# A redrawn opening: weights between the pieces of x on one load queue, and half of the token work moved into the loop

## The chip, the core and the metric

The kernel runs on one core of a Trainium2 chip. The metric is the device time of one execution in microseconds. The core has a matrix engine (PE, with its weight loads shown as PEld), a vector engine (DVE), a scalar engine (ACT), a general engine (POOL) and a queue engine (SP) that here issues all DMA transfers. Each engine runs its own instruction list in order, and waits on semaphores for the others.

## What is computed

One block of a Perceiver-like network on x (32 batches, 32 tokens, 256 features) with a context of 257 rows per batch. In float32:

```python
y  = layernorm(x)
Q  = y @ Wq.T + bq;  K = ctx @ Wk.T + bk;  V = ctx @ Wv.T + bv     # 16 heads of 16
x1 = x + (softmax(mask(Q K^T / 4)) V) @ Wo.T + bo
x2 = x1 + causal self attention with rotary positions (W_Q, W_K, W_V, W_O) of layernorm(x1)
out = x2 + top-2 mixture of 8 experts (gated, hidden 1368) of layernorm(x2)
```

The shapes and the use of x, of the context and of the eight square weights are what matters here. The expert part is not touched by the change.

## The kernel before, in words

The 1024 tokens are 8 tiles (TT) of 128 rows, 4 batches to a tile. Each float32 matrix product is made as three products (product3, lines 215 to 217) of a high and a low part: a transposed operand lands in a bank of PSUM, ACT rounds it into the high part, and DVE subtracts to get the low part.

The program has an opening, a loop of 8 steps (j) with 4 units (u) each, one unit for each batch b = 4j + u, a stage that routes tokens, and a stage for the experts. The change touches the opening and the first two steps of the loop.

**The opening before.** SP issues, in this order: the constant table, the four pieces of x (x_sb, 256 KB each), the first three weights (w_raw: Wq and Wk in two pieces of 128 KB each, because their rows are regrouped by head, lines 336 and 337; Wv in one), the last context rows, the three biases, the context of batches 0 to 3, bo, the mask, the other five weights, the router. PE takes a list of slots, each in one of 8 banks: the bias (line 435), the weights 0 to 2 (line 440), the last context rows (line 459), their keys and values (kl, vl), the four pieces of normed tokens (xT, line 446), and four query products (q) of 512 columns. ACT copies every slot (lines 935 to 949), and DVE makes the low parts of weights, last rows and tokens (line 1245). DVE clears three buffers first, then makes the statistics of all 8 tiles (lines 1250 to 1255), and POOL takes the power -0.5 (line 1756). DVE norms all tiles (line 1261). POOL adds bo to x (line 1761). Only after all slots are done does the context of batch 0 go through PE: turn_ctx (line 491), keys, values, then turn_ctx for batch 1.

**The loop before.** Unit b starts with energies(b) (line 534), then turns the context of b + 2, makes the keys of b + 1, turns probabilities of b - 1 (line 556), makes the values of b + 1, and in units 0 to 2 of step 0 turns two late weights (line 592), which ACT and DVE split (lines 954 and 1272). values(b + 1) waits until ACT has kept the keys (line 971), since both use bank 5. The scores of a unit are shifted by DVE (line 1296), exponentiated by ACT (line 994), and scaled by POOL (line 1799).

**vl.** The values of the last context row are stored to memory and read back eight times with a broadcast (VL_all, line 387, 1 MB written in all). SP issues the context of batch 4 only behind that.

## Time and profile before

| | |
|---|---|
| median of 3 runs | 563.48 us (556.87 to 567.03) |
| the profiled execution | 566.69 us, of which the trace spans 564.8 us |
| busy share of the span | PE 89%, DVE 72%, ACT 58%, POOL 44% |
| first energies (start of the loop) | 45.05 us after the span's start |
| PE busy in 0 to 45.05 us | 23.57 us |
| PE busy in 45.05 to 297 us | 237.20 of 251.95 us |

An execution's time is the span and some 2 us around it. PE is busy nearly all the time from the loop on, but only about half of the opening. A row of the timeline gives start, duration, engine, line, operation, output and inputs, shape and count, and in brackets how long the engine had been idle before it and what ended that. A row of the windows gives the stretch, its length, the busy time of each engine with the number of instructions, the granted PE clock (PEclk), the mean busy share of the 16 DMA engines and the GB/s moved.

### The profile page before, as it was taken

Reading aid. Unit: us, or ns where it says so; the run is one execution under the profiler, and the core shown is the slowest. Engines: PE = TensorE matmul, PEld = TensorE weight load, DVE = VectorE, ACT = ScalarE, POOL = GpSimd, SP = SyncE. Lnnn points to the kernel's source line nnn. Section 1 sums busy time; section 2 is a strip of 40 time slices with the busy share of each in tenths; the row PEclk is TensorE's granted clock in tenths of the full one; section 3 lists DMA queues with packets and bytes.
Section 4 is the critical chain, followed back from the end, with each engine's and each line's share of the span. In section 5 each row is a group of like instructions: output and inputs, shape, how many; then the busy total and the mean of one; then the engine's idle time right before and its main releaser. Section 6 shows DMA issues by size and latency. Waiting matters only on the chain.

```text
span 564.8 us, 18262 instructions
## 1 busy us (share of the span) xinstructions
PE 501.6 (89%) x6637; PEld 460.1 (81%) x6637; DVE 406.2 (72%) x1005; ACT 325.1 (58%) x839; POOL 247.3 (44%) x337
## 2 busy tenths in 40 slices
PE   0777999989999999999976657899999999999996
PEld 0656778878889898888865546799999999999995
DVE  6414346477666767676676788599999999999973
ACT  0325667577667757676752215666665766657650
POOL 1301153344445364444430120366667667676650
PEclk9989899999999999999996765599999999999998
DMA  7420111121111111120006200055655656465302
GB/s 217 129 94 19 38 43 40 27 55 22 42 39 35 26 33 38 21 54 2 4 2 200 102 0 1 5 196 167 188 158 189 198 174 195 146 187 188 113 1 74
DMA packets 57981, 48.91 MB, mean 87 GB/s; under 512 B 20926, under 2 KB 49600, under 8 KB 57920
## 3 DMA queue, kind: packets, MB, share of 16 engines
q1 hardware_dynamic: 57920, 48.09, 28.9%
q8 instruction: 39, 0.64, 0.5%
q14 instruction: 22, 0.18, 0.1%
HBM read 46.86 MB, written 1.08 MB: 85 GB/s over the span
## 4 chain that ended last, share of the span: by engine, by line
PE 77%; ACT 7%; DVE 5%; issue 5%; DMA 2%; SPq 2%; POOL 0%; DVEq 0%; ACTq 0%; POOLq 0%
PE bank L215 20%; PE bank L217 18%; PE bank L216 18%; PE bank L556 5%; PE bank L534 3%; PE bank L580 3%; ACT Pr L994 2%; PE bank L491 2%; PE bank L925 2%; PE bank L711 1%; ACT PTd L1087 1%; DMA bias_raw<-in_L_xattn_bv 1%; PE bank L673 1%; DMA last_prob<-Pr 1%; PE bank L684 1%
## 5 line engine op out<-in xcount | busy, mean ns | idle before, releaser
L215 PE MATMUL bank<-XT_lo,W_hi 128*128 128x256 f32 (+1 forms) x352 | 100.5, 286 | 1.3 <-ACT CT L1166 1.3
L216 PE MATMUL bank<-XT_hi,W_lo 128*128 128x256 f32 (+1 forms) x352 | 100.1, 284 | 0.0
L217 PE MATMUL bank<-XT_hi,W_hi 128*128 128x256 f32 (+1 forms) x352 | 99.8, 284 | 0.0
L1876 POOL TENSOR_TENSOR W_lo<-raw,W_hi 128x256 fp32r<-128x256 f32 (+1 forms) x88 | 88.4, 1005 | 7.0
L1799 POOL TENSOR_TENSOR Pr<-Pr,rinv 128x1028 f32<-128x1028 f32 x31 | 58.9, 1901 | 51.1 <-DVE rinv L1307 50.4
L994 ACT ACTIVATE Pr<-Sc,nmax 128x257 f32<-128x257 f32 x128 | 63.8, 502 | 23.1 <-DVE nmax L1296 21.6
L1296 DVE CUSTOM_DVE_ANT_0 Sc<-bank,mask_add 128x257 f32<-128x257 f32 x128 | 46.9, 422 | 38.8 <-PE bank L534 16.8
L1738 DVE TENSOR_TENSOR hid_lo<-hid,hid_hi 128x256 fp32r<-128x256 f32 (+1 forms) x88 | 73.1, 831 | 1.5 <-ACT hid_hi L1215 1.5
L1708 DVE TENSOR_TENSOR W_lo<-raw,W_hi 128x512 fp32r<-128x512 f32 (+1 forms) x88 | 68.8, 784 | 5.2 <-ACT W_hi L1139 1.4
L1874 POOL CAST W_hi<-raw 128x256 fp32r<-128x256 f32 (+1 forms) x88 | 39.1, 444 | 74.3 <-PE bank L217 36.9
L215 PEld LDWEIGHTS bank<-XT_lo,W_hi 128*128 128x128 f32 (+1 forms) x352 | 66.6, 189 | 1.6 <-issue 1.6
L216 PEld LDWEIGHTS bank<-XT_hi,W_lo 128*128 128x128 f32 (+1 forms) x352 | 66.4, 189 | 0.0
L217 PEld LDWEIGHTS bank<-XT_hi,W_hi 128*128 128x128 f32 (+1 forms) x352 | 66.3, 188 | 0.0
L1211 ACT ACTIVATE act<-bank 128x256 f32<-128x256 f32 (+1 forms) x88 | 33.7, 383 | 53.9 <-PE bank L217 53.3
L1139 ACT ACTIVATE W_hi<-raw 128x512 fp32r<-128x512 f32 (+1 forms) x88 | 53.6, 612 | 0.0
L215 PE MATMUL bank<-W_lo,hid_hi 128*128 128x256 f32 (+1 forms) x176 | 49.7, 282 | 0.5 <-issue 0.5
L216 PE MATMUL bank<-W_hi,hid_lo 128*128 128x256 f32 (+1 forms) x176 | 49.5, 281 | 0.0
L217 PE MATMUL bank<-W_hi,hid_hi 128*128 128x256 f32 (+1 forms) x176 | 49.5, 281 | 0.0
L1215 ACT ACTIVATE hid_hi<-hid 128x256 fp32r<-128x256 f32 (+1 forms) x88 | 36.9, 419 | 14.2 <-DVE hid L1733 12.3
L1733 DVE TENSOR_TENSOR hid<-bank,act 128x256 f32<-128x256 f32 (+1 forms) x88 | 36.4, 414 | 11.8 <-ACT act L1211 11.5
L215 PE MATMUL bank<-WT_lo,ctxT_hi 128*128 128x256 f32 x128 | 40.1, 314 | 4.7 <-ACT KT L971 4.5
L215 PE MATMUL bank<-ctxT_lo,WT_hi 128*128 128x256 f32 x128 | 39.4, 308 | 1.5 <-DVE ctxT_lo L1281 1.5
(234 smaller groups left out, 1333.4 us busy)
## 6 DMA issues: line engine op xcount, KB each, us to landing
raw<-in_L_ffn_w_kernel SPq DMA_DIRECT2D x32, 512.0 KB, 4.6
ctx_raw<-in_ctx SPq DMA_DIRECT2D x32, 256.0 KB, 2.8
raw<-in_L_ffn_wo_kernel SPq DMA_DIRECT2D x16, 512.0 KB, 5.8
raw<-in_L_ffn_w_kernel SPq DMA_DIRECT2D x16, 344.0 KB
last_prob<-Pr SPq DMA_DIRECT2D x128, 1.0 KB, 1.8
raw<-in_L_ffn_wo_kernel SPq DMA_DIRECT2D x8, 256.0 KB
x_sb<-in_x SPq DMA_DIRECT2D x4, 256.0 KB, 3.9
VL_all<-vl_rows SPq DMA_DIRECT2D x8, 128.0 KB
```

The lines of the kernel that those rows point to most:

```text
L215: pe.matmul(dst, a_hi, b_lo, start=first, stop=False)
L216: pe.matmul(dst, a_lo, b_hi, start=False, stop=False)
L217: return pe.matmul(dst, a_hi, b_hi, start=False, stop=last)
L994: ac.activation(Pr[:, r % 2, g, 0:SC], Sc[:, r % 2, g, 0:SC], ACT.Exp, bias=nmax[:, r % 2, g:g + 1], scale=-1.0, accum_out=Pr[:, r % 2, g, ...
L1139: ac.activation(W01_hi[:, (NT * half_ + n) % RW, :, :, 0:w].rearrange("p i k n -> p (i k) n"), raw01[:, :, :, t * P:t * P + w].rearrange(" ...
L1215: ac.activation(hid_hi[0:w, m % RW, :], hid[0:w, m % RH, :], ACT.Copy).then_inc(sm["hhi_done"], 1)
L1296: ve.tensor_tensor_reduce(Sc[:, r % 2, g, 0:SC], bk[g][:, 0:SC], mask_add[:, :], -0.25, 3e38, ALU.add, ALU.min, nmax[:, r % 2, g:g + 1]).t ...
L1708: ve.tensor_tensor(W01_lo[:, (NT * half_ + n) % RW, :, :, 0:w].rearrange("p i k n -> p (i k) n"), raw01[:, :, :, t * P:t * P + w].rearrang ...
L1738: ve.tensor_tensor(hid_lo[0:w, m % RW, :], hid[0:w, m % RH, :], f(hid_hi[0:w, m % RW, :]), ALU.subtract)\
L1799: po.tensor_tensor(Pr[:, r % 2, :, 0:SC], Pr[:, r % 2, :, 0:SC], rinv[:, r % 2, :].unsqueeze(2).broadcast_to([P, G, SC]), ALU.mult).then_i ...
L1874: po.tensor_copy(W2_hi[0:w, m % RW, :], raw2[0:w, t, :]).then_inc(sm["hi2"], 1)
L1876: po.tensor_tensor(W2_lo[0:w, m % RW, :], raw2[0:w, t, :], f(W2_hi[0:w, m % RW, :]), ALU.subtract)\
```

## The change

All loads stay on SP, but in another order: the identity part of the table alone, Wq, x pieces 0 and 1, Wk, the biases, the context of batch 0, Wv, the last rows, the rest of the table, the context of batch 1, the mask, x pieces 2 and 3, and so on.

The list of slots is shorter and in another order. Only tokens 0 to 511 (x pieces 0 and 1) are normed, turned and projected in the opening. The context of batch 0 is turned behind the first two weights, and its keys are made behind the third. The slots use six banks. The other half of the tokens is done by functions called late (PE, ACT, DVE) in unit 3 of step 0 and unit 0 of step 1. values(0) is made inside unit 0, behind energies(0). DVE no longer clears V, PTd and Vm: POOL does. POOL adds bo to x two tiles per unit of step 0. The late weights are turned ahead of values(b + 1) and no longer behind, and ACT splits them ahead of keep_values.

```diff
-    slots = [("bias", 0)] + [("w", i) for i in range(WF)] + [("lastT", 0), ("kl", 0), ("vl", 0)]
-    slots += [("xT", c) for c in range(4)] + [("q", c) for c in range(4)]
+    slots = [("w", 0), ("w", 1), ("bias", 0), ("lastT", 0), ("xT", 0), ("xT", 1), ("w", 2), ("q", 0), ("q", 1), ("kl", 0), ("vl", 0)]
+    ROOM = (0, 1, 2, 3, 6, 7)
...
+    def late_tokens(j, u, part):
+        return {(0, 3, 0): (0,), (0, 3, 1): (1,), (1, 0, 0): (2,), (1, 0, 1): (3,)}.get((j, u, part), ()) if isinstance(j, int) else ()
...
             elif kind == "vl":
+                pe.wait_ge(sm["first_act"], n)
+                pe.wait_ge(sm["first_dve"], sum(by_dve[:n]))
...
+        def late(n):
+            pe.wait_ge(sm["w_lo"], 8 - WF)
+            if n < 2:
+                pe.wait_ge(sm["lx_lo"], n)
+                turn_tokens(2 + n, bk[6]).then_inc(sm["lx_made"], 1)
+            else:
+                pe.wait_ge(sm["lx_hi"], 2)
+                pe.wait_ge(sm["lx_lo"], 2)
+                pe.wait_ge(sm["lq_kept"], n - 2)
+                queries(1, n - 2, bk[6]).then_inc(sm["lq_made"], 1)
...
+        for n in range(2):
+            prepare(n)
         turn_ctx(0, 0, 16)
+        for n in range(2, slot("w", 2) + 1):
+            prepare(n)
         keys(0, 0)
-        values(0, 0)
+        for n in range(slot("q", 0), slot("vl", 0)):
+            prepare(n)
         turn_ctx(1, 1, 16)
+        prepare(slot("vl", 0))
+        pe.wait_ge(sm["first_act"], NS)
+        pe.wait_ge(sm["first_dve"], sum(by_dve))
...
                 energies(b, u)
+                if isinstance(j, int) and b == 0:
+                    values(0, 0)
...
-                values(b + 1, (u + 1) % 4)
                 for i in late_weights(j, u):
                     turn_weight(i)
+                for n in late_tokens(j, u, 1):
+                    late(n)
+                values(b + 1, (u + 1) % 4)
...
+        po.memset(V[:, :, :, :, :], 0.0).then_inc(sm["v_zero"], 1)
         po.wait_ge(sm["ones_set"], 1)
+        for part in range(2):
+            tiles = slice(TT // 2 * part, TT // 2 * (part + 1))
+            po.wait_ge(sm["ln1_var"], part + 1)
+            po.tensor_tensor(rstd[:, tiles], mv[:, tiles, 1], half[:, tiles], ALU.pow).then_inc(sm["ln1_rstd"], 1)
+            if part == 0:
+                po.memset(PTd[:, :, :, :, :], 0.0)
+                po.memset(Vm[:, :, :, :], 0.0).then_inc(sm["diag_zero"], 1)
```

On PE, the opening. Before, every slot comes ahead of the context of batch 0 (waits in brackets: w_in is a weight's load, ctx_in a context's, last_in the last rows', ln1_done the normed tokens, first_act and first_dve the slots that ACT and DVE are done with):

```order
L435 MATMUL bank<-tab,bias_raw 128x6 [waits bias_in,const_in]
L440 MATMUL bank<-tab,w_raw 128x128 [waits w_in0]
...
L459 MATMUL bank<-tab,last_raw 128x32 [waits last_in]
...
L215 MATMUL bank<-lastT_lo,WT_hi 128x32 [waits first_dve,first_act]
...
L446 MATMUL bank<-tab,xn 128x128 [waits ln1_done]
...
L215 MATMUL bank<-xnT_lo,WT_hi 128x512 [waits first_act,first_dve]
...
L491 MATMUL bank<-tab,ctx_raw 128x128 [waits ctx_in0,first_dve,first_act]
...
L215 MATMUL bank<-ctxT_lo,WT_hi 128x256 [waits ctx_lo,ctx_hi]
```

And now:

```order
L474 MATMUL bank<-tab,w_raw 128x128 [waits w_in0,const_in]
...
L474 MATMUL bank<-tab,w_raw 128x128 [waits w_in1]
...
L541 MATMUL bank<-tab,ctx_raw 128x128 [waits ctx_in0]
...
L469 MATMUL bank<-tab,bias_raw 128x6 [waits bias_in]
L485 MATMUL bank<-tab,last_raw 128x32 [waits last_in]
...
L506 MATMUL bank<-tab,xn 128x128 [waits ln1_done]
...
L474 MATMUL bank<-tab,w_raw 128x128 [waits w_in2,first_dve,first_act]
...
L223 MATMUL bank<-ctxT_lo,WT_hi 128x256 [waits ctx_lo,ctx_hi]
...
L223 MATMUL bank<-xnT_lo,WT_hi 128x512 [waits first_act,first_dve]
...
L223 MATMUL bank<-lastT_lo,WT_hi 128x32 [waits first_act,first_dve]
...
L541 MATMUL bank<-tab,ctx_raw 128x128 [waits ctx_lo,ctx_hi,ctx_in1]
...
L223 MATMUL bank<-WT_lo,lastT_hi 32x256 [waits first_act,first_dve]
```

The bias has left the head of the list, two of four query pieces are gone from it, and the context of batch 0 stands in the middle.

On DVE, the opening. Before, behind the three memsets:

```order
L1250 BN_STATS bn<-x_sb 128x6 [waits x_in3]
L1250 BN_STATS bn<-x_sb 128x6
L1253 BN_AGGR mv<-bn 128x2 [waits ln1_stats]
L1253 BN_AGGR mv<-bn 128x2 x7
L1255 TENSOR_SCALAR mv<-mv 128x8 [waits ln1_stats]
L1245 TENSOR_TENSOR WT_lo<-bank,WT_hi 128x512 [waits first_act] x3
L1245 TENSOR_TENSOR lastT_lo<-bank,lastT_hi 128x64 [waits first_act]
L1261 TENSOR_SCALAR xn<-x_sb,mv,rstd 128x256 [waits ln1_rstd]
L1261 TENSOR_SCALAR xn<-x_sb,mv,rstd 128x256 x7
```

And now:

```order
L1338 BN_STATS bn<-x_sb 128x6 [waits x_in1]
L1338 BN_STATS bn<-x_sb 128x6
L1341 BN_AGGR mv<-bn 128x2 [waits ln1_stats]
L1341 BN_AGGR mv<-bn 128x2 x3
L1344 TENSOR_SCALAR mv<-mv 128x4 [waits ln1_stats]
L1330 TENSOR_TENSOR WT_lo<-bank,WT_hi 128x512 [waits first_act] x2
L1351 TENSOR_SCALAR xn<-x_sb,mv,rstd 128x256 [waits ln1_rstd]
L1351 TENSOR_SCALAR xn<-x_sb,mv,rstd 128x256 x3
L1378 TENSOR_TENSOR ctxT_lo<-bank,ctxT_hi 128x512 [waits ctx_hi]
L1330 TENSOR_TENSOR lastT_lo<-bank,lastT_hi 128x64 [waits first_act]
L1330 TENSOR_TENSOR xnT_lo<-bank,xnT_hi 128x2x256 [waits first_act] x2
```

Four tiles are normed where eight were, and they still stand behind a weight's low part, now Wk's.

On SP, the head of the queue. Before:

```order
L341 DMA tab<-in_table 128x682
L344 DMA x_sb<-in_x 128x2x256 x4
L337 DMA w_raw<-in_L_xattn_Wq 128x1x256 x2
L337 DMA w_raw<-in_L_xattn_Wk 128x1x256 x2
L339 DMA w_raw<-in_L_xattn_Wv 128x2x256
```

And now:

```order
L359 DMA tab<-in_table 128x128
L353 DMA w_raw<-in_L_xattn_Wq 128x1x256 x2
L363 DMA x_sb<-in_x 128x2x256 x2
L353 DMA w_raw<-in_L_xattn_Wk 128x1x256 x2
L375 DMA bias_raw<-in_L_xattn_bq 2x4x32
L375 DMA bias_raw<-in_L_xattn_bk 2x4x32
L375 DMA bias_raw<-in_L_xattn_bv 2x128
L379 DMA ctx_raw<-in_ctx 128x2x256
L355 DMA w_raw<-in_L_xattn_Wv 128x2x256
```

Half of x and most of the table have moved behind the weights, and one context has moved ahead of Wv.

## Rows read from the trace of the kernel before

**Rows 1.** The page, the chain that ended last, by engine

```profile
PE 77%; ACT 7%; DVE 5%; issue 5%; DMA 2%; SPq 2%; POOL 0%; DVEq 0%; ACTq 0%; POOLq 0%
```

**Rows 2.** Timeline of PE, the opening

```profile
15.48 0.24 PE L435 MATMUL bank<-tab,bias_raw 6*128 6x6 f32 x1 [15.48 <-DMA bias_raw<-in_L_xattn_bv]
15.65 2.82 PE L440 MATMUL bank<-tab,w_raw 128*128 128x128 f32 x12
...
23.92 3.62 PE L446 MATMUL bank<-tab,xn 128*128 128x128 f32 x16
...
35.66 0.66 PE L491 MATMUL bank<-tab,ctx_raw 128*128 128x128 f32 x4 [0.78 <-ACT QT L942]
...
45.05 0.69 PE L534 MATMUL bank<-KT,Qb 32*64 32x257 f32 x16
```

**Rows 3.** The chain in order of time, the load that PE waits for

```profile
8.81 6.53 DMA bias_raw<-in_L_xattn_bv
```

**Rows 4.** Windows around four groups of products on PE

```profile
20.10:23.92 3.82, 3.81 (x18) 3.60 (x19) 2.44 (x8) 0.47 (x2) 1.21 (x2) 1.00 0.62 187
29.04:34.88 5.84, 5.83 (x24) 4.41 (x24) 0.06 (x1) 2.06 (x3) 0.00 (x0) 1.00 0.26 88
37.82:40.55 2.73, 2.73 (x12) 2.44 (x12) 0.00 (x0) 0.00 (x0) 0.00 (x0) 0.53 0.47 155
47.01:48.67 1.66, 1.66 (x15) 1.45 (x13) 1.54 (x7) 1.66 (x6) 0.00 (x0) 1.00 0.19 67
```

**Rows 5.** Windows: the rate of the loads

```profile
3.00:4.00 1.00, 0.00 (x0) 0.00 (x0) 1.00 (x1) 0.00 (x0) 0.00 (x0) 1.00 1.04 366
17.00:18.00 1.00, 1.00 (x6) 1.00 (x6) 0.57 (x1) 0.74 (x2) 0.00 (x0) 1.00 0.27 88
29.00:35.00 6.00, 5.83 (x24) 4.43 (x24) 0.10 (x1) 2.15 (x4) 0.00 (x0) 1.00 0.26 88
```

**Rows 6.** Timeline of DVE, the opening

```profile
7.92 2.65 DVE L1250 BATCH_NORM_STATS2 bn<-x_sb 128x6 f32<-128x256 f32 x8
10.60 0.64 DVE L1253 BATCH_NORM_AGGREGATE mv<-bn 128x2 f32<-128x6 f32 x8
...
17.43 0.69 DVE L1245 TENSOR_TENSOR WT_lo<-bank,WT_hi 128x512 fp32r<-128x512 f32 x1 [5.99 <-ACT WT_hi L937]
...
19.88 2.66 DVE L1261 TENSOR_SCALAR xn<-x_sb,mv,rstd 128x256 f32<-128x256 f32 x8
```

**Rows 7.** Timeline of POOL, the opening

```profile
11.60 1.65 POOL L1756 TENSOR_TENSOR rstd<-mv,half 128x8 f32<-128x8 f32 x1 [11.14 <-DVE mv L1255]
22.71 5.52 POOL L1761 TENSOR_TENSOR x_sb<-x_sb,bo_row 128x256 f32<-128x256 f32 x8 [9.46 <-DVE xn L1261]
```

**Rows 8.** Timeline of ACT, a slot of queries kept

```profile
34.92 0.69 ACT L942 ACTIVATE QT<-bank,bias_col 128x512 f32<-128x512 f32 x1 [0.71 <-PE bank L217]
```

**Rows 9.** Timeline of PE, units 0 to 2 of step 0

```profile
50.19 0.39 PE L215 MATMUL bank<-WT_lo,ctxT_hi 128*128 128x256 f32 x1 [1.52 <-ACT KT L971]
...
51.72 1.04 PE L592 MATMUL bank<-tab,w_raw 128*128 128x128 f32 x8
52.69 0.69 PE L534 MATMUL bank<-KT,Qb 32*64 32x257 f32 x16
...
56.45 1.09 PE L556 MATMUL bank<-tab,Pr 128*128 128x128 f32 x8 [1.08 <-POOL Pr L1799]
...
62.18 0.69 PE L534 MATMUL bank<-KT,Qb 32*64 32x257 f32 x16
```

**Rows 10.** Timeline of DVE, unit 1 of step 0

```profile
53.04 1.29 DVE L1272 TENSOR_TENSOR WT_lo<-bank,WT_hi 128x512 fp32r<-128x512 f32 x2 [4.37 <-ACT WT_hi L954]
```

**Rows 11.** Timeline of SP's queue: VL_all and the context behind it

```profile
27.15 6.69 SPq L387 DMA_DIRECT2D VL_all<-vl_rows  x8
36.35 9.18 SPq L365 DMA_DIRECT2D ctx_raw<-in_ctx  x2
```

**Rows 12.** DMA issues at 36.3 us, with time to landing

```profile
ctx_raw<-in_ctx SPq DMA_DIRECT2D x1, 256.0 KB, 5.0
```

More of the change, by code:

```diff
@@ L429, in _, with prepare @@
         pe.wait_ge(sm["const_in"], 16)
-        for n, (kind, i) in enumerate(slots):
-            dst = bk[n % 8]
+        def prepare(n):
+            kind, i = slots[n]
+            dst = slot_bank(n)
             free_slot(pe, n)
@@ L930, in _, with prepare @@
     def _(ac):
-        for n, (kind, i) in enumerate(slots):
-            src = bk[n % 8]
+        def prepare(n):
+            kind, i = slots[n]
+            src = slot_bank(n)
             ac.wait_ge(sm["first_made"], n + 1)
@@ L1089, in spread_probs, with late @@
             last.then_inc(sm["b_pT_act"], 1)
+        def late(n):
+            if n < 2:
+                ac.wait_ge(sm["lx_made"], n + 1)
+                ac.activation(xnT_hi[1][:, :, n * D:(n + 1) * D], halves(bk[6]), ACT.Copy).then_inc(sm["lx_hi"], 1)
+            else:
+                ac.wait_ge(sm["lq_made"], n - 1)
+                ac.activation(QT[:, n - 2, 512:1024], bk[6], ACT.Identity, bias=bq_col[:, n - 2:n - 1]).then_inc(sm["lq_kept"], 1)
+        for n in range(2):
+            prepare(n)
         split_ctx(0, 0)
+        for n in range(2, slot("w", 2) + 1):
+            prepare(n)
+        ac.wait_ge(sm["first_act"], slot("bias", 0) + 1)
         keep_keys(0, 0)
-        keep_values(0, 0)
+        for n in range(slot("q", 0), slot("vl", 0)):
+            prepare(n)
         split_ctx(1, 1)
+        prepare(slot("vl", 0))
         def step(j):
@@ L1107, in step @@
                 exps(b, u, (1, 2, 3))
+                for n in late_tokens(j, u, 0):
+                    late(n)
                 if u == 0:
@@ L1122, in step @@
                     split_self(j - 2)
+                for i in late_weights(j, u):
+                    split_weight(i)
+                for n in late_tokens(j, u, 1):
+                    late(n)
                 keep_values(b + 1, (u + 1) % 4)
@@ L1227, in _, with low @@
         ve.memset(half[:, :], -0.5).then_inc(sm["ones_set"], 1)
-        ve.memset(V[:, :, :, :, :], 0.0).then_inc(sm["v_zero"], 1)
-        ve.memset(PTd[:, :, :, :, :], 0.0)
-        ve.memset(Vm[:, :, :, :], 0.0).then_inc(sm["diag_zero"], 1)
-        def low(n, kind, i):
+        def low(n):
+            kind, i = slots[n]
             ve.wait_ge(sm["first_act"], n + 1)
-            src = bk[n % 8]
+            src = slot_bank(n)
             if kind == "w":
@@ new lines, in norm_tokens, with set_mask @@
+        def norm_tokens(part):
+            ve.wait_ge(sm["ln1_rstd"], part + 1)
+            for n in range(TT // 2):
+                j = TT // 2 * part + n
+                ve.tensor_scalar(xn[part][:, n, :], x_sb[:, j, :], mv[:, j, 0:1], rstd[:, j:j + 1], ALU.subtract, ALU.mult)\
+                  .then_inc(sm["ln1_done"], 1)
+        def set_mask():
+            ve.wait_ge(sm["mask_in"], 64)
+            ve.wait_ge(sm["table_in"], 16)
+            ve.tensor_scalar(mask_add[:, :], mask_i[:, :], 0.0, MASKED * 4.0, ALU.is_equal, ALU.mult).then_inc(sm["maskb_set"], 1)
@@ L1567, in weigh @@
             ve.tensor_tensor(tile_of(C_all, t), tile_of(C_all, t), second[:, :], ALU.add).then_inc(sm["r_weighed"], 1)
+        statistics(0)
+        low(slot("w", 0))
+        low(slot("w", 1))
+        norm_tokens(0)
         split_ctx(0, 0)
+        low(slot("lastT", 0))
+        low(slot("xT", 0))
+        low(slot("xT", 1))
+        low(slot("w", 2))
+        statistics(1)
+        set_mask()
         split_ctx(1, 1)
+        norm_tokens(1)
         ve.wait_ge(sm["maskb_set"], 1)
@@ L1591, in step @@
                 split_ctx(b + 2, u)
+                for n in late_tokens(j, u, 0):
+                    late(n)
                 if u == 0:
@@ L1606, in step @@
                     split_weight(i)
+                for n in late_tokens(j, u, 1):
+                    late(n)
                 if isinstance(j, int) and j == TT - 1:
@@ L1834, in _ @@
         spread(0, 0)
-        po.wait_ge(sm["xbo_done"], TT)
         def step(j):
```

208 lines of the change are left out of this document (116 added, 92 removed).

## The prediction

> **What bounds the kernel now.** I read the chain that ended last first: PE holds 77% of it [rows 1]. From the loop on PE is busy nearly all the time, so whatever is taken off before the first energies should come off the end, if the loop keeps its pace. Next I read PE's timeline in the opening. PE does nothing until 15.48 us, and what ends that is the load of the last bias, issued at 8.81 and landed 6.53 later, at 15.34 [rows 2, 3]. All slots run from there, the first context is turned only at 35.66, and the first energies stand at 45.05 [rows 2]. That number, called E0 below, is what the change is about.
>
> Then PE's pace. 18 products of the last rows take 3.82 us, 0.212 each. 24 query products of 512 columns take 5.84, 0.243 each. 12 key products of 256 columns take 2.73 at a granted clock near 0.5, the 1.2 GHz level, and 1.66 at 1.00, the 2.4 GHz level [rows 4]. So the same key group costs 2.73 or 1.66. The clock column shows 1.00 for the first two groups too, but the early 128 by 128 transposes take 2.82 for 12 and 3.62 for 16 [rows 2], 0.23 each, and 8 of them in the loop take 1.04 [rows 9], 0.13 each. I believe the durations: the opening ran at the lower level until about the queries, then high (512 columns in 0.243), then low again from the first keys. PE had worked from 20.1 to 27.5 almost without a stop before it rose.
>
> Last, the loads. With x on the way 366 GB/s flow and all DMA engines are busy. At 17 us, with only by-head weights left, it is 88 GB/s at a busy share of 0.27, as if four of sixteen engines worked; the same while VL_all is read (share 0.26, 88 GB/s) [rows 5]. A by-head weight (262 KB) is thus 2.9 us on four engines, on which a quarter of every other load lies too.
>
> **The opening, step by step.** First the loads. The bias landed at 15.34 behind a quarter of table, x, Wv and last rows (421 KB) and all of Wq and Wk (524 KB) on those four engines: 945 KB in 13.5 us from the first data at about 1.8 (my choice, 1 us behind the first issue), 70 GB/s. At 70, Wq lands at 5.8, x pieces 0 and 1 at 7.6, Wk at 11.4. At 88, with nothing in the way, Wk is there at 9.3. I take 10.8 for Wk (nearer to 70, since that includes such mixing), 11.2 for the biases, 12.1 for context 0, 12.9 for Wv and the last rows. Context 1, the mask and the rest of x land at 15 to 17, ahead of their use.
>
> DVE's statistics, without the memsets, follow x: four tiles are half of 2.65 and of 0.64 [rows 6], done at 8.9. POOL's power takes 1.65 [rows 7], so 10.6. POOL clears V before that: 3072 elements per partition at the pace of its bias addition (0.69 us for 256) would be 8.3 us, done at 8.7. That is hidden, and costs up to 2 us more before it shows. PTd and Vm (3584 elements, at most 9.7 us) end by 20.3, ahead of POOL's next use near 24.
>
> Wk is the late one. PE turns it until 11.75, ACT rounds it until 12.45, DVE subtracts (0.69 [rows 6]) until 13.15, and only then norms four tiles, half of 2.66: 14.5. PE has meanwhile turned context 0 and the last rows. The first pair of tiles is normed at 13.8, so two token pieces are turned until 15.6 and Wv until 16.5, 0.23 a transpose. Keys of batch 0 at the lower level: 2.6, until 19.1. By then PE has worked since 13.9 without a stop, and I take the higher level from there. Queries: 12 products at 0.24, 2.8, until 21.9. The list then has kl wait until ACT has kept the second query, 0.94 in the same place before (0.78 of idle and the flow of signals [rows 2, 8]): 22.8. kl is 12 short products. No row has them at the higher level; bounds are 0.125 (256 columns high) and 0.212 (low). I take 0.125, as their weight loads are those of the other products: 24.3. Context 1 until 24.8, vl (6 products) until 25.7, ACT's copy of it until 26.2. **E0 = 26.3**, where it was 45.05: 18.8 us less. The gain is three things: the start on Wq and x and not on the bias, half of the token work gone, and the context's chain of PE, ACT, DVE laid beside the slots.
>
> **Unit 0.** values(0) now stands behind energies(0), 1.4 us at the higher level. Before, PE idled 0.9 here, so keys(1) and ACT's work come 0.9 later. But the late weights now stand in front of values(1), where PE idled 1.52 for the kept keys [rows 9]; their 1.0 us goes into that hole. The two cancel, and unit 0 stays at 7.6.
>
> **Units 1 and 2.** Before, DVE's two low parts at 53.04, 1.29 long [rows 10], stood ahead of the maxima of unit 1, and POOL's scaling was late, so that PE idled 1.08 at 56.45 [rows 9]. Now they are ready a unit's tail earlier: 1.0 of that chain goes, and the next two transposed weights fill the hole before values(2). Unit 1 took 9.49 (52.69 to 62.18), some 1.7 of it because the clock had dropped at 58.5. I expect 6.1 to 7.8. With 0.7 off unit 2 the three units give 2.4 to 4.1; I take 3.2.
>
> **The late tokens.** 8 transposes (1.0) and 12 query products (2.8) are put into two units in which PE idles little, 1.1 in all before the values. They cost 2.7; 3.8 without that cover. ACT's four and DVE's two extra instructions have idle time on either side. POOL's bias additions, 1.4 us per unit, come after each scaling and fit before the next Qb.
>
> **Where a stall goes.** Context 4 is issued behind VL_all. Before, the eight issues began at 27.15, the context was issued at 36.35 and landed 5.0 later, 41.35 [rows 11, 12], 16.9 behind the copy of vl. Now the late weights are out of the way by then, so 16.1: 42.3. PE wants it 0.6 into unit 2, at E0 + 14.3 = 40.6, because the units before are shorter. PE, ACT and DVE wait behind it: 1.7 us, 0 to 3. Both times hang on vl, so a later E0 does not cure it.
>
> **Sum**: 18.8 + 3.2 - 2.7 - 1.7 = 17.6. Against the profiled execution 566.7 - 17.6 = 549.1; the same ratio on the median is 546.0. The three runs before spread over 10 us, so I take 548.
>
> **The rivals.**
> *The lower level stays (0.15).* PE has holes in the new opening: a few transposes at 6, then nothing until 10.9. If it rises only in the loop, queries take 0.427 each (512 columns at the pace of 256 in 0.213), 5.1, kl 2.6, context 0.9, vl 1.3: E0 = 30.4, and values(0) costs 1.2 more. Gain 12.4, 554 by the profile, 551 by the median. For it: PE worked 7.4 us before it rose the first time. Against: that work was mostly products with 32 columns. The Trainium skill, "TensorE: Matmul & The Clock Gate", section on the HAM clock gate, says that the throttled clock is the default and that sustained activity releases it. By that rule alone this rival is the one to fear, with its 551 to 554; the trace agrees that levels fall after idle stretches.
>
> *The loop gives nothing back (0.13).* Units 0 to 2 keep their length, 0.9 is lost in unit 0, the late tokens cost 3.8, the stall 3: 18.8 - 0.9 - 3.8 (stall gone if units are long) = 14.1, or 11.1 with both. 553 to 556 by the profile.
>
> *Wk lands early (0.07).* At 9.3 the opening is 1.5 shorter, bounded by the power at 10.6: gain 19, 545 by the median. The Trainium skill, "DMA: Bandwidth & Descriptors", on how many engines a DMA uses, says that the slowest dimension sets the engine count, which gives 4 for the by-head pieces; it speaks against putting Wq ahead of x, since x then waits for those four. The busy share of 0.27 agrees. Its price is in the sum.
>
> *Slower (0.03).* If the shorter loads and the stall at context 4 leave PE at the lower level in the loop, a group of keys costs 1.1 more, and a unit with four such groups' worth about 4 to 5. Four units at that level would eat 17.6, and seven would make it slower by 2%. In the loop before it fell once for some 3 us, so this is unlikely.
>
> **Chances.** Forecast 0.60, 541 to 552. The rest (0.02) is a POOL memset slower than any row. What can be told from no change is about 2%, 11.3 us, so faster needs 552.2. The forecast and early Wk are faster; the lower level is so in half of its cases, the loop case in a third. That is 0.60 + 0.07 + 0.08 + 0.04 and a little off for the spread of runs: faster 0.78, same 0.19, slower 0.03. The range 541 to 556 leaves out the far ends.
>
> **What would show it.** First energies at 24 to 29. PE's first long wait ended by Wk, not by the bias. The order Wk, low part, normed tiles, token transposes without a hole between 13 and 20. Unit 1 under 8 us. A wait of PE on ctx_raw at the start of unit 2. If the queries take 0.43 each, the first rival holds. I am wrong if E0 is over 31, or if the units of step 0 and 1 grow by more than 6 us together.

## The result and the profile after

The changed kernel takes 554.07 us (median; 552.16 to 558.19), the kernel before took 564.63 beside it (556.87 to 567.36). The ratio of the runs counted as fast is 0.986, with a 95% interval of 0.983 to 0.988, and that of the two medians is 0.981. By the first the change makes the kernel faster by 1.2 to 1.7%, by the second by 1.9%: clear of zero, and short of 2%. The forecast was 548.0, and a gain of over 2%. The time lies inside the range of 541 to 556, near its slow end.

The profiled execution took 554.86 us, its span is 553.1. Beside before's span of 564.8 that is 11.7 us less, where the sum had 17.6. The chain that ended last, by engine, answers to [rows 1] and has the same shape:

```profile
PE 79%; ACT 6%; DVE 5%; issue 5%; DMA 3%; SPq 1%; DVEq 0%; ACTq 0%; POOL 0%; POOLq 0%
```

PE's timeline of the opening, which answers to [rows 2] (start, duration, engine, line, operation, in brackets the idle time ahead and what ended it):

```profile
7.32 1.08 PE L474 MATMUL bank<-tab,w_raw 128*128 128x128 f32 x4 [7.32 <-DMA w_raw<-in_L_xattn_Wq]
12.54 1.12 PE L474 MATMUL bank<-tab,w_raw 128*128 128x128 f32 x4 [4.14 <-DMA w_raw<-in_L_xattn_Wk]
...
15.71 1.97 PE L506 MATMUL bank<-tab,xn 128*128 128x128 f32 x8 [0.59 <-DVE xn L1351]
17.47 1.06 PE L474 MATMUL bank<-tab,w_raw 128*128 128x128 f32 x4
18.18 0.56 PE L223 MATMUL bank<-ctxT_lo,WT_hi 128*128 128x256 f32 x1
...
23.89 0.25 PE L223 MATMUL bank<-lastT_lo,WT_hi 128*128 128x32 f32 x1 [0.97 <-ACT QT L1007]
...
26.13 0.39 PE L223 MATMUL bank<-WT_lo,lastT_hi 128*32 128x256 f32 x1 [0.18 <-issue]
...
28.05 1.17 PE L584 MATMUL bank<-KT,Qb 32*64 32x257 f32 x16 [0.46 <-ACT vl L1014]
```

The long wait is now Wq and then Wk, not the bias, and the first energies stand at 28.05 where they stood at 45.05: 17.0 us less. The chain in order of time shows Wk's load, which answers to the bias of [rows 3]:

```profile
4.23 8.26 DMA w_raw<-in_L_xattn_Wk
```

On DVE, behind Wk's low part, the norms follow without a hole, in 1.37 us for four tiles (half of the 2.66 of [rows 6]); the statistics had waited for x until 7.87:

```profile
7.87 1.56 DVE L1338 BATCH_NORM_STATS2 bn<-x_sb 128x6 f32<-128x256 f32 x4 [6.82 <-DMA x_sb<-in_x]
...
14.32 0.69 DVE L1330 TENSOR_TENSOR WT_lo<-bank,WT_hi 128x512 fp32r<-128x512 f32 x1 [3.68 <-ACT WT_hi L1003]
14.93 1.37 DVE L1351 TENSOR_SCALAR xn<-x_sb,mv,rstd 128x256 f32<-128x256 f32 x4
```

POOL's memsets, which answer to [rows 7], take far less than the 8.3 and 9.7 us that I had allowed them:

```profile
0.75 2.66 POOL L1866 MEMSET V<- 128x3072 f32 x1 [0.29 <-POOLq L2025]
...
11.16 1.80 POOL L1873 MEMSET PTd<- 128x2048 f32 x1
12.90 1.38 POOL L1874 MEMSET Vm<- 128x1536 f32 x1
```

Then PE in the first five units of the loop, which answers to [rows 9]:

```profile
35.94 0.39 PE L223 MATMUL bank<-WT_lo,ctxT_hi 128*128 128x256 f32 x1 [0.54 <-ACT KT L1036]
37.56 0.69 PE L584 MATMUL bank<-KT,Qb 32*64 32x257 f32 x16
43.94 0.69 PE L584 MATMUL bank<-KT,Qb 32*64 32x257 f32 x16
47.23 0.66 PE L541 MATMUL bank<-tab,ctx_raw 128*128 128x128 f32 x4 [2.60 <-DMA ctx_raw<-in_ctx]
53.84 0.69 PE L584 MATMUL bank<-KT,Qb 32*64 32x257 f32 x16
61.15 0.69 PE L584 MATMUL bank<-KT,Qb 32*64 32x257 f32 x16
69.71 0.69 PE L584 MATMUL bank<-KT,Qb 32*64 32x257 f32 x16
```

The wait for the kept keys has shrunk from 1.52 to 0.54, and the 1.08 for POOL is gone, as forecast. New is a wait of 2.60 us for the context of batch 4. SP's queue shows what lies ahead of it, as in [rows 11]:

```profile
31.10 6.73 SPq L418 DMA_DIRECT2D VL_all<-vl_rows  x8
37.87 1.93 SPq L388 DMA_DIRECT2D ctx_raw<-in_ctx  x2
39.85 2.80 SPq L396 DMA_DIRECT2D last_prob<-Pr  x4
```

The last line is four copies of 1 KB: the last probabilities of unit 0 on their way to last_prob. ACT may not overwrite their buffer with the exponentials of unit 2 (line 1059) before they have landed, and that took 6.73 us for the last of them. ACT waits 4.23 us, and the split of context 4 stands behind that exponential in its list. ACT's timeline and the chain that ended last:

```profile
48.88 0.51 ACT L1059 ACTIVATE Pr<-Sc,nmax 128x257 f32<-128x257 f32 x1 [4.23 <-DMA last_prob<-Pr]
```

```profile
42.04 6.73 DMA last_prob<-Pr
```

So two transfers stand behind VL_all and are wanted in unit 2. Context 4 lands at 47.2, the copies at 48.8, and the chain goes through the copies.

The windows (length, busy time of PE, PEld, DVE, ACT, POOL with counts, then granted clock, DMA share, GB/s) show where PE's clock stood, beside the groups of [rows 4]:

```profile
18.90:25.70 6.80, 5.83 (x39) 4.94 (x37) 2.90 (x12) 2.77 (x7) 1.02 (x1) 1.00 0.48 146
25.70:32.50 6.80, 6.15 (x39) 4.56 (x38) 3.45 (x13) 1.53 (x4) 2.92 (x8) 0.50 0.09 26
32.50:44.80 12.30, 11.34 (x111) 9.39 (x109) 6.29 (x17) 10.30 (x30) 3.86 (x6) 1.00 0.46 128
```

The clock column shows 1.00 before 18.9 as well, so PE's rise is read from the key products: 0.22 us each until then, 0.118 from there. The queries thus ran as fast as I had taken them. But PE is back at 1.2 GHz, this time in the column too, from 25.7 to 32.5: over the turn of context 1, vl, energies(0) and values(0).

The account, by the starts of energies (before's from the timeline of before, E0 to E5 at 45.05, 52.69, 62.18, 69.45, 76.63, 83.05):

| | before | after | change | forecast |
|---|---|---|---|---|
| to energies(0) | 45.05 | 28.05 | -17.0 | -18.8 |
| unit 0 | 7.64 | 9.51 | +1.9 | 0 |
| unit 1 | 9.49 | 6.38 | -3.1 | -1.7 to -3.4 |
| unit 2 | 7.27 | 9.90 | +2.6 (2.60 of it the wait) | -0.7 + 1.7 |
| units 3 and 4 | 13.60 | 15.87 | +2.3 | +2.7 |
| lead at energies(5) | | | 13.3 | 17.6 |
| from there to the end | 481.75 | 483.39 | +1.6 | 0 |
| the span | 564.8 | 553.1 | -11.7 | -17.6 |

### The profile page after: what moved, and what is told of

It is laid out like the page before. It is cut to its first block, busy times and chain, and to the rows that moved or that the text cites. A ratio compares the mean times of both kernels' runs of the same rounds, so it can differ in the third digit from the quotient of the medians.

```text
span 553.1 us, 18277 instructions
## 1 busy us (share of the span) xinstructions
PE 497.3 (90%) x6637; PEld 455.6 (82%) x6637; DVE 400.3 (72%) x1003; ACT 324.7 (59%) x839; POOL 253.9 (46%) x341
## 3 DMA queue, kind: packets, MB, share of 16 engines
HBM read 46.86 MB, written 1.08 MB: 87 GB/s over the span
## 4 chain that ended last, share of the span: by engine, by line
PE 79%; ACT 6%; DVE 5%; issue 5%; DMA 3%; SPq 1%; DVEq 0%; ACTq 0%; POOL 0%; POOLq 0%
PE bank L223 20%; PE bank L225 18%; PE bank L224 18%; PE bank L606 5%; PE bank L584 4%; PE bank L630 3%; PE bank L541 2%; ACT Pr L1059 2%; DMA last_prob<-Pr 2%; PE bank L989 2%; DMA w_raw<-in_L_xattn_Wk 1%; PE bank L761 1%; ACT PTd L1152 1%; PE bank L723 1%; PE bank L734 1%
## 5 line engine op out<-in xcount | busy, mean ns | idle before, releaser
L1845 DVE TENSOR_TENSOR hid<-bank,act 128x256 f32<-128x256 f32 (+1 forms) x88 | 36.5, 414 | 11.9 <-ACT act L1298 11.7
L1412 DVE COPY PT<-bank 128x512 f32<-128x512 f32 x32 | 22.1, 691 | 24.5 <-PE bank L606 24.2
```

## The experiments

Two theories at the outset. **Placed by context 4:** what units 0 to 2 save is taken back by the wait for context 4, whose landing hangs on vl and on the eight VL_all transfers, so neither the clock nor the order on PE changes where unit 3 starts. **Placed by PE:** the low clock in unit 0 and the late E0 are what is missing, and each comes off the end when mended. A third theory came only from reading ACT: **placed by the copies.** The 1 KB copies to last_prob, issued behind context 4 on the same queue, hold ACT's exponential of unit 2. No run was made to part the last from the first; the traces of all of them are read for it below.

Below, "start of unit n" is the start of energies(n), and every ratio is to the kernel before, run beside it. That kernel's median was 567.17 beside the first four experiments, 563.47 beside the next four and 562.88 beside the last, so small differences between ratios of different groups say little, and the starts of units in the traces say more.

**One: the by-head weights regrouped.** Each of them is now four transfers of 32 partitions and not two transfers whose outer dimension is 4. Nothing else changes in the kernel after.

```diff
-    src = weights[i].rearrange("(r c x) n -> c r x n", r=HG, c=KH)
-    for c in range(KH):
-        eng.dma_start(w_raw[:, i, c, :], src[c]).then_inc(w_in[i], 16)
+    src = weights[i].rearrange("(r c x) n -> r x c n", r=HG, c=KH)
+    for r in range(HG):
+        eng.dma_start(w_raw[r * S:(r + 1) * S, i, :, :], src[r]).then_inc(w_in[i], 16)
```

> The changed kernel, with each by-head weight (Wq, Wk, W_Q, W_K) loaded in four transfers of 32 partitions, whose outer dimension is 32, where it was two transfers whose outer dimension is 4. Theory (loads on four DMA engines set the opening): Wk, which ended PE's wait at 12.54, is there by about 8.5, the DMA share no longer stands near 0.27 but near 1 while weights are loaded, the first energies come near 24 where they were at 28.05, and the time falls by 3 to 4 us. Rival (the chain of DVE and POOL or SP's issue time sets it): four issues a weight at 0.5 us put later loads back by as much, and the first energies stay within 1 us of 28.

Measured: 551.9 us (550.16 to 554.39) against 567.17, ratio 0.972 (0.967 to 0.978). Wq is there at 4.69 and Wk at 8.03, 4.5 us earlier than in the kernel after, and E0 is 25.14. Only 2.9 of the 4.5 reach E0; where the rest went shows under the third experiment. Unit 0 still takes 9.51, and the wait for context 4 is still 2.54: unit 3 starts at 50.86, 3.0 earlier. Since vl is earlier, context 4 is too, and so are the copies to last_prob (ACT's exponential of unit 2 starts at 45.89 and not at 48.88).

**Two: VL_all regrouped.** Four transfers by b, each with 32 partitions outside, for eight by j with 4 outside.

```diff
-    for j in range(TT):
-        src = vl_rows[BT * j:BT * j + BT, :].unsqueeze(1).broadcast_to([BT, S, D])
-        sp.dma_start(VL_all[:, j, :], src).then_inc(sm["vl_in"], 16)
+    rows_of = vl_rows.rearrange("(j b) d -> b j d", b=BT)
+    for b in range(BT):
+        src = rows_of[b].unsqueeze(0).broadcast_to([S, TT, D])
+        sp.dma_start(VL_all[b * S:(b + 1) * S, :, :], src).then_inc(sm["vl_in"], 16)
```

> The changed kernel, with the values of the last context row read back in four transfers of 32 partitions and 8 tiles each, where it was eight transfers whose outer dimension is 4. Theory (the wait of 2.60 us for context 4 comes from 1 MB on four DMA engines ahead of it): VL_all takes some 3 us and not 15, PE's wait on the context load is gone, the time falls by 2.6 us. Rival (the wait is only moved: what PE does next waits for ACT or POOL at that point): the load is early but less than 1 us is won.

Measured: 552.1 us (549.13 to 555.12) against 567.17, ratio 0.972 (0.965 to 0.979). PE's timeline in units 2 and 3 and SP's queue:

```profile
44.53 0.69 PE L585 MATMUL bank<-KT,Qb 32*64 32x257 f32 x16
45.15 0.66 PE L542 MATMUL bank<-tab,ctx_raw 128*128 128x128 f32 x4
...
50.95 0.69 PE L585 MATMUL bank<-KT,Qb 32*64 32x257 f32 x16
```

```profile
31.80 1.81 SPq L419 DMA_DIRECT2D VL_all<-vl_rows  x4
33.65 0.96 SPq L388 DMA_DIRECT2D ctx_raw<-in_ctx  x2
```

No wait at the context: unit 2 takes 6.42 and not 9.90, and unit 3 starts at 50.95, though E0 was 0.6 later than in the kernel after. The price of the two late transfers is thus some 3.5 us, of which PE's bracket showed 2.60. ACT doesn't wait for last_prob here either: the copies land in 1.8 to 2.0 us where the last took 6.73, and the exponential starts at 45.98. Of the experiments on the kernel after that leave E0 about where it was (this one and the fifth), only this one brings unit 3 forward.

**Three: both, on the kernel after.**

> Both of the former in the changed kernel. If the two are independent, the sum: 5.6 to 6.6 us less than the changed kernel, near 546 to 548. If the earlier opening only runs into another wait in the loop, no more than the larger of the two.

Measured: 550.96 us (547.97 to 551.05) against 567.17, ratio 0.971 (0.967 to 0.976). E0 is 25.86 and unit 5 starts at 63.72, 6.0 before that of the kernel after (69.71), so in the trace the two add up (2.96 and 2.90 by themselves). The times of one, two and three stand closer to each other than this, 551.9, 552.1 and 551.0, and their intervals overlap: how much the second regrouping adds to the first in the time isn't settled.

DVE's first norm and POOL's memsets, in this kernel:

```profile
10.32 2.18 DVE L1352 TENSOR_SCALAR xn<-x_sb,mv,rstd 128x256 f32<-128x256 f32 x1
```

```profile
9.23 1.81 POOL L1874 MEMSET PTd<- 128x2048 f32 x1
10.98 1.38 POOL L1875 MEMSET Vm<- 128x1536 f32 x1
```

Here is the rest of the 4.5 us. A norm takes 0.41 by itself; this first one started in the middle of a memset and ended at 12.50, when the second memset was over (12.36). The four norms took 3.15 us and not 1.37, and the tokens were turned at 12.87. In the kernel after the norms begin at 14.93, behind both memsets (14.28), so it cost nothing there.

**Four: both, on the kernel before.** This asks how much of the change's gain lies in something that it does not touch.

> The kernel before the change, with both regroupings of its loads. Theory: the bias that PE waits for stands behind Wq and Wk on four engines and lands at 12 instead of 15.3, so the time falls by 2 to 4 us. Context 4 is not waited for there, so the regrouping of VL_all adds nothing. Rival: SP's own issue time (two more issues a weight, 1 us each) takes the place of the transfers, and the time stays within 1 us.

Measured: 559.49 us (557.29 to 564.04) against 567.17, ratio 0.987 (0.980 to 0.995). The same two diffs, on the old order of slots, give about what the whole redrawn opening gave (0.986), and more than the 2 to 4 us expected. PE's timeline:

```profile
10.98 0.24 PE L436 MATMUL bank<-tab,bias_raw 6*128 6x6 f32 x1 [10.98 <-DMA bias_raw<-in_L_xattn_bv]
...
37.56 0.69 PE L535 MATMUL bank<-KT,Qb 32*64 32x257 f32 x16
```

The bias, still behind Wk, is there 4.5 us earlier, and E0 comes 7.5 earlier. Of the further 3.0, 2.6 lie between the turn of context 0 and E0 (9.4 before, 6.8 here): by the durations PE's clock rises in the token transposes, near 21.7 (16 of them take 3.05 us, before 3.62), and stays, where before it fell at the first keys ([rows 4], 2.73 for the key group).

**Five: the late weights behind values(b + 1) again.** On the kernel after; the same on ACT.

```diff
-                for i in late_weights(j, u):
-                    turn_weight(i)
                 for n in late_tokens(j, u, 1):
                     late(n)
                 values(b + 1, (u + 1) % 4)
+                for i in late_weights(j, u):
+                    turn_weight(i)
```

> The changed kernel, with the late weights turned behind values(b + 1) again, and split by ACT behind keep_values, as before the change. Theory (the prediction's: the late weights fill PE's hole before the values and take DVE's low parts off the path of the next unit): unit 0 grows by 1 us, unit 1 from 6.38 to about 8, and the load of context 4, which is late by 2.60, is waited for less by the same amount, so that the first energies of unit 3 move by under 1 us. Rival (the holes were not the price): units 0 and 1 keep their length.

Measured: 554.79 us (550.46 to 556.65) against 563.47, ratio 0.982 (0.975 to 0.990). In PE's timeline the two holes of [rows 9] are back:

```profile
35.94 0.39 PE L223 MATMUL bank<-WT_lo,ctxT_hi 128*128 128x256 f32 x1 [1.43 <-ACT KT L1036]
...
42.20 1.09 PE L606 MATMUL bank<-tab,Pr 128*128 128x128 f32 x8 [1.08 <-POOL Pr L1919]
```

Units 0 and 1 are 10.38 and 7.93, so the new place of the late weights saves 0.9 in unit 0 and 1.6 in unit 1, as argued. But unit 2 is 7.65 with no wait for context 4, and unit 3 starts at 54.02, against 53.84: of the 2.4 us saved, 2.2 are taken back. That speaks for the transfers and against PE as what places unit 3. And it speaks for the copies over context 4: PE does not wait for context 4 here, yet ACT still waits 1.44 us for last_prob and starts its exponential at 48.61, beside 48.88 in the kernel after.

**Six: values(0) between the queries and kl.** This removes the 0.97 us stop ahead of the 32-column products, and puts wide products there.

```diff
-                if isinstance(j, int) and b == 0:
-                    values(0, 0)
...
+        for n in range(slot("q", 0), slot("kl", 0)):
+            prepare(n)
...
+        values(0, 0)
+        prepare(slot("kl", 0))
```

> The changed kernel, with values(0) made between the queries and the keys of the last rows (kl), where PE stood idle 0.97 us for ACT, and no longer behind the first energies. Theory A (PE falls to its lower level at 25.7 because it stops and then runs products of 32 columns; 1.4 us of wide products there keep it up): no stretch at 0.5 before the loop, unit 0 near 6.5 where it was 9.51, first energies 0.5 to 1 us later, sum 2 to 3 us less, of which the wait for context 4 takes back none, since it hangs on vl. Theory B (the thin products behind alone bring it down): the level still falls for some 7 us, just later, unit 0 near 8, sum 0 to 1 us less.

Measured: 556.6 us (554.41 to 557.38) against 563.47, ratio 0.986 (0.980 to 0.992). Windows and PE's timeline:

```profile
25.70:32.50 6.80, 6.00 (x60) 4.85 (x59) 4.05 (x14) 4.09 (x13) 2.94 (x8) 1.00 0.11 34
...
44.80:51.60 6.80, 4.51 (x79) 4.12 (x80) 0.69 (x1) 2.56 (x9) 1.36 (x4) 0.50 0.39 102
```

```profile
28.84 0.69 PE L584 MATMUL bank<-KT,Qb 32*64 32x257 f32 x16 [0.46 <-ACT vl L1016]
35.26 0.69 PE L584 MATMUL bank<-KT,Qb 32*64 32x257 f32 x16
...
47.09 1.12 PE L541 MATMUL bank<-tab,ctx_raw 128*128 128x128 f32 x4 [4.77 <-DMA ctx_raw<-in_ctx]
```

Until 44.8 the clock stays at 2.4 GHz, and unit 0 takes 6.42 and not 9.51, for an E0 that is 0.8 later. So the low clock is real and cost unit 0 about 1.7, beside the 1.4 of values(0) itself. Yet unit 3 starts at 54.60, later than the 53.84 of the kernel after: the wait at context 4 has grown to 4.77 (ACT's for last_prob to 6.36), and in the midst of it PE fell to the lower level for 6.8 us. I had expected that the wait would take back none of this gain; it took all of it.

**Seven: the kernel after with the load order of before.** Table, all of x, three weights, last rows, biases, contexts, with the new slots.

```diff
-        load_weight(sp, 0)
-        load_x(0)
-        load_x(1)
-        load_weight(sp, 1)
+        sp.dma_start(tab[:, P:NC_], table[:, P:NC_]).then_inc(sm["table_in"], 16)
+        for i in range(TT // 2):
+            load_x(i)
+        for i in range(WF):
+            load_weight(sp, i)
+        sp.dma_start(last_raw[:, :], ctx_in[:, SC - 1, :]).then_inc(sm["last_in"], 16)
```

> The changed kernel, with its loads issued in the order of before: whole table, four pieces of x, Wq, Wk, Wv, last rows, biases, four contexts, mask. Theory (the order of the loads is what lets the opening start early): Wk lands at 14 and the last rows at 14.9 as before, where Wk was there at 12.5; the first energies come 1.5 to 2.5 us later. Rival (the order hardly matters, since the four engines have the same bytes to bring before Wk): within 0.5 us. By bytes, 945 KB lie before the bias in the old order and 671 KB before Wk in the new one.

Measured: 556.81 us (554.02 to 559.56) against 563.47, ratio 0.988 (0.981 to 0.996). Wq comes at 10.72, Wk at 14.98, E0 at 30.87. PE at context 4 and at unit 3:

```profile
48.20 0.66 PE L536 MATMUL bank<-tab,ctx_raw 128*128 128x128 f32 x4 [0.74 <-DMA ctx_raw<-in_ctx]
...
54.81 0.69 PE L579 MATMUL bank<-KT,Qb 32*64 32x257 f32 x16
```

The new order of loads is worth 2.8 us at E0, 1.0 at unit 3, and nothing that the times can tell (0.988 beside 0.986). Most of the change's 17.0 at E0 is thus the order of slots and the half of tokens, with little from the interleaved loads.

**Eight: the kernel before with the biases loaded right behind the table.** It prices the bias at the head of the list.

> The kernel before the change, with the three bias loads issued right behind the table. Theory (the prediction's: the bias behind everything sets the start, but Wk and Wv stand right behind it): PE starts on Wq near 10.4, but Wk comes at 14.0 and Wv and the last rows at 14.9, so kl, the norms and all that follows come 2 to 3 us earlier and not 5. Rival (the chain from the statistics sets it): under 1 us.

Measured: 562.12 us (560.03 to 564.23) against 563.47, ratio 0.998 (0.995 to 1.000). PE's timeline:

```profile
3.96 0.24 PE L435 MATMUL bank<-tab,bias_raw 6*128 6x6 f32 x1 [3.96 <-DMA bias_raw<-in_L_xattn_bv]
10.79 1.12 PE L440 MATMUL bank<-tab,w_raw 128*128 128x128 f32 x4 [6.59 <-DMA w_raw<-in_L_xattn_Wq]
14.56 1.97 PE L440 MATMUL bank<-tab,w_raw 128*128 128x128 f32 x8 [2.66 <-DMA w_raw<-in_L_xattn_Wk]
```

The bias hid a second wait right behind it: with the bias gone, Wk is waited for until 14.56, only 1.1 us before the weights started in [rows 2]. E0 is 41.54, 3.5 earlier, and in the time hardly anything can be told. I had expected 2 to 3 at E0.

**Nine to twelve: what the traces point to.** Four versions of the kernel after, run together against 562.88 of before:

> The changed kernel with VL_all read back on all DMA engines and with values(0) ahead of kl. Theory (context 4 had swallowed what values(0) ahead of kl won): no wait for context 4, unit 0 at 6.4 where it was 9.51, first energies at 29.4, first energies of unit 3 at 48 where they were at 50.95 with the read-back alone. 2.9 us less than that kernel. Rival (the level falls somewhere else in its place): unit 3 starts at 50 or later.

> The changed kernel with both regroupings of loads, and POOL clears PTd and Vm at once behind V and not behind the first power. Theory (DVE's four norms took 3.15 us where they had taken 1.37 because POOL's memsets ran beside them): they take 1.4 again, and the first energies come 1.5 us earlier than 25.86. Rival (they waited for the power or for x): they stay near 3.

> All of it: both regroupings, POOL's memsets first, values(0) ahead of kl. If the terms add: first energies near 25, unit 0 at 6.4, no wait for context 4, unit 3 near 44 and unit 5 near 60, where the changed kernel had 53.84 and 69.71. 8 to 10 us less than the changed kernel, 3 to 4 less than the one with both regroupings alone.

> The same, and DVE norms the first four tiles ahead of the low part of Wk, with the tokens turned ahead of the last rows. If Wk is still what the norms wait for, another 0.5 to 1.5 us off the first energies. If the chain from x through statistics and power is as late as Wk by now, nothing.

The third edit, used here for the first time, has POOL clear all three buffers ahead of its first wait:

```diff
         po.memset(V[:, :, :, :, :], 0.0).then_inc(sm["v_zero"], 1)
+        po.memset(PTd[:, :, :, :, :], 0.0)
+        po.memset(Vm[:, :, :, :], 0.0).then_inc(sm["diag_zero"], 1)
...
-            if part == 0:
-                po.memset(PTd[:, :, :, :, :], 0.0)
-                po.memset(Vm[:, :, :, :], 0.0).then_inc(sm["diag_zero"], 1)
```

| kernel after, with | us | ratio, 95% | E0 | unit 0 | start of unit 5 |
|---|---|---|---|---|---|
| VL_all regrouped, values(0) ahead of kl | 550.34 | 0.974 (0.967 to 0.981) | 29.20 | 6.42 | 64.30 |
| both regrouped, memsets first | 545.43 | 0.969 (0.963 to 0.975) | 24.29 | 9.51 | 62.47 |
| all four edits | 543.40 | 0.964 (0.957 to 0.970) | 24.69 | 6.42 | 59.77 |
| the four, norms ahead of Wk's low part | 543.41 | 0.966 (0.961 to 0.971) | 23.94 | 6.41 | 59.02 |

With the memsets first, the four norms of the second version take their own time again:

```profile
10.38 1.38 DVE L1352 TENSOR_SCALAR xn<-x_sb,mv,rstd 128x256 f32<-128x256 f32 x4
```

and E0 comes 1.6 earlier than in experiment three. The version with all four edits beats both kernels: 543.4 us, PE at 2.4 GHz from 16.5 on through the whole opening and loop, and no wait for context 4 or last_prob in unit 2. Its PE timeline:

```profile
24.69 0.69 PE L585 MATMUL bank<-KT,Qb 32*64 32x257 f32 x16 [0.46 <-ACT vl L1017]
31.11 0.69 PE L585 MATMUL bank<-KT,Qb 32*64 32x257 f32 x16
```

With the two waits behind VL_all out of the way, values(0) ahead of kl is worth 2.7 at the start of unit 5 (62.47 to 59.77) and about 2 in the time, though these two intervals overlap. On its own, in experiment six, unit 5 came 0.8 later and the ratio was that of the kernel after. The last version moves E0 by a further 0.75 and the time not at all.

## Why the prediction was right in kind and wrong in size

**The steps that failed.** At unit 5 the lead was 13.3 us and not 17.6. The terms of units 0 to 2 (3.2 saved, 1.7 lost in the stall, so 1.5 to the good) came out as 1.4 lost: 2.9 us. E0 gave 17.0 and not 18.8: 1.8 us. The late tokens were 0.4 better. Three steps of the prediction are behind it: Wk's landing at 10.8, the higher clock level "from there" on, and the stall, priced for one load that PE wants and subtracted as a term of its own. Behind unit 5 the sum had nothing, and there more was lost.

**Much of the mechanism held.** PE's first long wait is for weights, the chain from Wk to low part, norms and token transposes is unbroken on PE and DVE, the context's chain lies beside the slots, and the holes in units 0 and 1 are filled. Of 17.6 us forecast 13.3 were there at unit 5.

**The loads were 1.7 us too early.** I chose 10.8 for Wk; it was 12.5. Everything behind it followed as worked out: the norms at 16.3 (forecast 14.5), Wv turned by 18.2 (16.5). The rate was the reason: 671 KB on the four engines by 12.5 us are 63 GB/s from the 1.8 us that I had chosen as the start, below both rates that I chose between. With Wq's pieces on their way and x just issued, hardly anything moved:

```profile
3.00:4.00 1.00, 0.00 (x0) 0.00 (x0) 0.00 (x0) 0.00 (x0) 0.41 (x1) 1.00 0.19 29
```

That is 29 GB/s where [rows 5] has 88 for such pieces; no run tells why. The keys caught up some 0.8, since the clock rose in their midst and not behind them, and vl at the lower level lost it again. Hence E0 28.05 and not 26.3. I had said that the slow rate comes from by-head weights, four engines each, and costed it between two rates; experiment one shows what it is worth: with the weights on more engines, Wk is there at 8.0. The Trainium skill, "DMA: Bandwidth & Descriptors", section on why a DMA increments its semaphore by 16, says that the largest number up to 16 that divides the slowest dimension of both sides is the number of engines used. The traces agree: 4 outside goes with a DMA share of 0.27 and 88 GB/s [rows 5], and with 32 outside context 4 lands soon enough behind VL_all that PE never waits. I had read that rule, and used it only to place a price, not to ask what sits behind the four engines later.

**Unit 0 took 9.5 and not 7.6.** I took the higher level "from there" on, once it had risen. It rose about where I said and fell again at 25.7, after 0.97 us without work, 12 products of 32 columns and a short transpose. The low level cost context 1 and vl some 0.7 ahead of E0, and unit 0 is 1.9 over its forecast. The rival "the lower level stays" had priced values(0) at that level (+1.2), but for a clock that never rose, so it had the wrong place: the queries ran at 0.23 each. Experiment six shows it from the other side: with values(0) in front of kl the level holds through the opening and units 0 and 1. It takes away the stop and puts wide products in at once, so which of the two holds the level isn't told apart; the thin products are in it as before. Against this rival I had also said that PE's 7.4 us of work before the first rise were mostly products with 32 columns. That was misread: 12 of them took 2.6 us of it, and products of 256 columns and 16 transposes took the rest.

**The wait for context 4 was 2.6 and not 1.7, and it isn't the wait that counts.** I had its place and cause right, treated it as one more term to subtract, and overlooked the copies to last_prob behind it on the queue. The traces show what sets the start of unit 3:

| kernel | E0 | units 0 and 1 | PE's wait for context 4 | ACT's wait for last_prob | ACT's exponential of unit 2 | start of unit 3 |
|---|---|---|---|---|---|---|
| after | 28.05 | 15.9 | 2.60 | 4.23 | 48.88 | 53.84 |
| late weights behind values | 28.06 | 18.3 | none | 1.44 | 48.61 | 54.02 |
| values(0) ahead of kl | 28.84 | 12.8 | 4.77 | 6.36 | 48.70 | 54.60 |
| old order of loads | 30.87 | 15.9 | 0.74 | 2.38 | 49.85 | 54.81 |
| weights regrouped | 25.14 | 15.9 | 2.54 | 4.16 | 45.89 | 50.86 |
| VL_all regrouped | 28.64 | 15.9 | none | none | 45.98 | 50.95 |

In four of the six, unit 3 starts 4.96 or 4.97 behind ACT's exponential. It is 5.41 where the late weights stand behind the values, and 5.90 where PE is at its lower level. Behind PE's turn of context 4 it is 6.6 in three of those four and 5.8 in the last, so context 4 is not what unit 3 follows. An estimate: with those 5.8 (45.15 to 50.95) from 47.23 on, context 4 alone would give 53.0, and the copies make it 53.8. No run mends one of the two transfers without the other. The first four differ by 2.8 us in E0 and 5.5 in units 0 and 1, and by 1.0 in what comes of it. So the 3.2 us that I added for units 0 to 2 could not be earned: what they save stands in front of a transfer that comes at its own time. I had even written that context 4 and E0 both hang on vl, so that a later E0 doesn't cure the wait; the turn of it, that shorter units lengthen it nearly us for us, I left out of the sum. I also had the landing 16.1 us behind the copy of vl. It was 19.2 (28.0 to 47.2): SP issued the context right behind VL_all, where 2.5 us lay between the two in [rows 11], so that the 5.0 us of [rows 12] did not carry over to a queue that was still full. Nor is the landing a fixed time behind vl: counted from the first issue of VL_all it is 16.1 us in the kernel after, 15.7 in experiment six and 15.8 in seven, but the store of the vl rows ahead of that took 3.1, 2.6 and 1.5. That is why E0 differs by 2.8 between the first and the last of these, and unit 3 by 1.0.

**The late tokens cost 2.3, forecast 2.7.** Right, and the steadiest term: 15.9 us for units 3 and 4 in every version of the new loop but the fifth experiment (16.4).

**Behind unit 5 some of the lead was lost again, and the sum had no term for it.** From energies(5) to the end the profiled execution of before took 481.75, that of after 483.39, and those of experiments one to seven between 482.2 and 485.9. Part of it is the stage that routes tokens (64.5 in before, 65.3 to 66.7 in after and in those seven), where PE's granted clock goes up and down. One profile of each kernel can't part chance from effect: a later version has 480.93. But the times point the same way. In each of the twelve versions of the experiments, as in the kernel after, the gain by the ratio is less than the lead at unit 5 over before's profile, by 0.6 to 5.8 us, in the kernel after 8.1 of 13.3. Experiment eight changes nothing in the loop, leads by 5.1 and gains 1.4. So about 3 us, and 5.3 in the kernel after, are missing between the lead and the time; the cause stays open, and that before's one profiled opening was a slow one isn't ruled out.

**The rival that came nearest** is "the loop gives nothing back", 553 to 556 by the profile with a chance of 0.13: units 0 to 2 took 25.8 where before took 24.4, and the wait was near its 3. Its time was close, its weight too small. Part of that is luck: it let the units keep their length and the late tokens cost 3.8, where unit 0 grew, unit 1 shrank and the tokens cost 2.3. "Slower" had nothing for it, and Wk was late, not early. What I had set up as proof of being wrong, E0 over 31 or five units longer by over 6, did not happen (28.05, and 3.7): those bounds were too wide to notice that a third of the gain was missing. And the step from the sum to the chances failed too. The bar for a gain of over 2% was 552.2, 6 us above the sum on the same scale (546.0) and 4 above the forecast, with five terms of 1 to 3 us each that I had picked between bounds, and none for the rest of the kernel; 0.78 was too much for that.

## What to carry to other kernels

Before a sum of savings is made, look for the load or copy that lands at its own time and is wanted behind them, on every engine and not only on the busiest: here PE's bracket named context 4, and the later transfer held ACT. Terms add up only as far as that wait, and behind it only what moves the landing counts. Look at the outer dimension of every transfer, since two regroupings here did as much as a redrawn opening. And an edit that gives nothing alone, as values(0) in its new place, may give its full price once the wait behind it is gone, so try it again then.
